# A decoder's second self-attention with four heads side by side in tiles of 32 rows, and one ring of four PSUM banks for scores and outputs in both self-attentions

## The reference

```python
# layer 0: 16 heads of 16 features, rotary positions, causal
p = softmax(where(causal, (q @ k.T) * 16 ** -0.5, -inf));  out = p @ v
# layer 1: differential attention, 16 heads, each of two half heads of 8 features
scores = einsum('bthd,bshd->bhts', qh, kh) * SCALE;  p = softmax(scores, axis=-1)
attn1, attn2 = attend(q1, k1), attend(q2, k2)          # same v for both
a = attn1 - lam * attn2;  a = a * rsqrt(mean(a * a, -1) + RMS_EPS) * rms_weight
```

## Time and profile before

| | us |
|---|---|
| runs | 3790.27, 3794.53 (median), 3812.66 |
| the profiled execution | 3793.69 |
| its span, first to last instruction | 3792.0 |
| first self-attention, from the first maximum matmul to the last reciprocal L678 | 144.1 to 629.89 |
| second self-attention, from the first reduction to the last reciprocal L678 | 1297.91 to 2641.81 |

### The profile page before, as it was taken

The page is one execution under the profiler, slowest core; times in us unless marked ns, Lnnn a source line. Parts: engine busy times, 40 slices in busy tenths (PEclk is TensorE's granted clock), DMA queues, the critical chain, the costliest instruction groups (busy, mean ns, idle before and its releaser), DMA issues. The chain is left out here.

```text
span 3792.0 us, 63919 instructions
## 1 busy us (share of the span) xinstructions
PE 3304.4 (87%) x23832; PEld 1646.7 (43%) x23832; DVE 2877.6 (76%) x4740; ACT 2100.6 (55%) x4079; POOL 912.5 (24%) x1343
## 2 busy tenths in 40 slices
PE   8499999686798799999999999999647599998748
PEld 4244444443686433333333333333424355544625
DVE  7688883467577999999999999996545377775475
ACT  3178886254232278888888888889412133333110
POOL 4233433144334300000000000000224434444000
PEclk9699998787899889999999999999778799999679
DMA  5322220000002500000100000010002311000202
GB/s 176 117 53 53 60 62 5 23 1 1 24 1 64 160 10 24 22 19 19 27 19 19 22 24 19 19 27 2 4 20 108 116 47 47 24 24 4 95 19 79
DMA packets 77548, 157.14 MB, mean 41 GB/s; under 512 B 21336, under 2 KB 38752, under 8 KB 77120
## 3 DMA queue, kind: packets, MB, share of 16 engines
q1 hardware_dynamic: 73024, 148.97, 13.1%
q10 hardware_dynamic: 4224, 4.19, 0.3%
HBM read 87.76 MB, written 54.72 MB: 38 GB/s over the span
## 5 line engine op out<-in xcount | busy, mean ns | idle before, releaser
L584 ACT ACTIVATE L_parts<-L_attn_psS 128x512 f32<-128x512 f32 (+3 forms) x2816 | 1442.6, 570 | 221.2 <-PE L_attn_psS L711 193.3
L667 DVE TENSOR_REDUCE L_attn_tops<-L_attn_psM 128x2 f32<-128x1024 f32 x1152 | 1397.8, 1222 | 95.1 <-PE L_attn_psM L761 85.1
L761 PE MATMUL L_attn_psM<-L_K,L_Q 62*128 62x512 f32 (+3 forms) x2816 | 996.4, 454 | 60.9 <-DVE L_attn_tops L667 26.8
L711 PE MATMUL L_attn_psS<-L_Q,L_K 64*128 64x512 f32 (+3 forms) x2816 | 1002.8, 439 | 1.4 <-ACT L_parts L584 1.0
L732 PE MATMUL L_attn_psO<-L_parts,L_attn_V 128*32 128x256 f32 (+1 forms) x10752 | 850.1, 388 | 20.2 <-ACT L_attn_oT L605 19.4
L711 PEld LDWEIGHTS L_attn_psS<-L_Q,L_K 64*128 64x128 f32 x2816 | 432.3, 187 | 534.7 <-ACT L_parts L584 467.5
L761 PEld LDWEIGHTS L_attn_psM<-L_K,L_Q 62*128 62x128 f32 x2816 | 415.8, 191 | 106.2 <-DVE L_attn_tops L667 58.3
L732 PEld LDWEIGHTS L_attn_psO<-L_parts,L_attn_V 128*32 128x32 f32 x10752 | 212.2, 108 | 473.7 <-issue 247.1
L661 DVE CUSTOM_DVE_ANT_0 L_attn_psM<-L_attn_psM,L_attn_wide 128x384 f32<-128x384 f32 (+3 forms) x512 | 236.6, 523 | 21.3 <-PE L_attn_psM L761 20.8
L2296 ACT ACTIVATE x_E<-x_psS 128x512 f32<-128x512 f32 x256 | 138.9, 595 | 178.4 <-PE x_psS L2419 165.7
L2342 DVE TENSOR_REDUCE x_tops<-x_psM 128x2 f32<-128x1024 f32 x128 | 153.2, 1206 | 90.0 <-PE x_psM L2448 89.9
(11 more groups left out here) (343 smaller groups left out, 4035.6 us busy)
## 6 DMA issues: line engine op xcount, KB each, us to landing
parts_q<-L_parts SPq DMA_DIRECT2D x64, 256.0 KB
parts_k<-L_parts SPq DMA_DIRECT2D x64, 256.0 KB
L_Q<-parts_q SPq DMA_DIRECT2D x192, 64.0 KB
L_K<-parts_k SPq DMA_DIRECT2D x192, 64.0 KB
L_Q<-parts_q SPq DMA_DIRECT2D x64, 128.0 KB
L_K<-parts_k SPq DMA_DIRECT2D x64, 128.0 KB
queries<-x1p_qo SPq DMA_DIRECT2D x16, 512.0 KB
keys<-x1p_ko SPq DMA_DIRECT2D x16, 512.0 KB
```

Source lines behind the costliest of these rows:

```text
L584: act.activation(E[(4 * n + s) % (4 * RING)][:, c0:], psS[bank][:, c0:], ACT.Exp, scale=scale).then_inc(e_done, 1)
L667: dve.tensor_reduce(dst, src, AX, ALU.max).then_inc(m_read, 1)
L711: pe.matmul(psS[bank][:, c0:], K[g.slot][r:r + RH, c, kt * P:(kt + 1) * P], Q[g.slot][r:r + RH, c, q * HALF + c0:(q + 1) * HALF], start=Tr ...
L761: last = pe.matmul(psM[bank][:, j * HALF:j * HALF + n], Q[t.slot][r:r + TOP, c, qt * P:(qt + 1) * P], K[t.slot][r:r + TOP, c, h * HALF:h * ...
```

## The change

Three edits, in `load_group` and `attend`.

1. In the second layer `RH` is 32: the four heads of a group lie at partitions 0, 32, 64 and 96 of chunk 0; chunk 1 is not used. `TOP` becomes 30, so a `most` contracts 30 rows instead of 62, a `score` 32 instead of 64. The DMAs are as many and as large.
2. In the second layer the list of maxima pairs alternates between heads (2, 3) and (0, 1), so that the two `most` of a half step lie on the two heads whose scores are not being made in it: scores 0, 1 go with maxima 3, 2, and scores 2, 3 with maxima 1, 0.
3. In both layers `psO` is gone and `psS` has four banks. The output sums take a bank of the ring like any other item ("O" in `taken`), hold it over a half of the queries and give it back (`left`) with the copy L605 (now L621), which counts in `e_done`. Every item takes the bank that was given back four places before it, and waits for that one count. `o_out` is gone.

```diff
@@ load_group
         for s in range(4):
-            c, r = s // 2, 64 * (s % 2)
+            rows = 64 if dh > 8 else 32
+            c, r = s * rows // P, s * rows % P
@@ attend
-    RH = 64
+    RH = 64 if causal else 32
...
-    for s in (0, 2):
-        for t, h in blocks:
-            keys = (t + 1) * P if causal else S
-            n = min(HALF, keys - h * HALF)
-            pairs.append((s, t, h, n, causal and h * HALF + n == keys))
+    order = [(s, at) for s in (0, 2) for at in blocks] if causal else [(s, at) for at in blocks for s in (2, 0)]
+    for s, (t, h) in order:
+        keys = (t + 1) * P if causal else S
+        n = min(HALF, keys - h * HALF)
+        pairs.append((s, t, h, n, causal and h * HALF + n == keys))
...
-        psS = [m.ps(f"{tag}_attn_psS{k}", HALF) for k in range(3)]
-        psO = m.ps(f"{tag}_attn_psO", HALF)
+        psS = [m.ps(f"{tag}_attn_psS{k}", HALF) for k in range(4)]
...
+                summed = (g - 1, n - LATE - BACK) if n >= LATE + BACK else (g - 2, NS + n - LATE - BACK)
+                live = 0 <= at[0] < groups
+                if live:
+                    left += [at + (s,) for s in range(4)]
+                    taken += [at + (s,) for s in range(2)]
+                if 0 <= summed[0] < groups and (summed[1] == 0 or summed[1] - 1 in ends):
+                    taken.append(("O", summed[0], steps[summed[1]][0]))
+                if live:
+                    taken += [at + (s,) for s in range(2, 4)]
...
+                if 0 <= summed[0] < groups and summed[1] in ends:
+                    left.append(("O",) + (summed[0], steps[summed[1]][0]))
...
+        bank_of = {}
+        for k, key in enumerate(taken):
+            bank_of[key] = k if k < 4 else bank_of[left[k - 4]]
+        order = {key: k for k, key in enumerate(taken)}
+        freed = {key: 4 + k + 1 for k, key in enumerate(left)}
...
-                    act.activation(oT[q][:], psO[:], ACT.Copy).then_inc(o_out, 1)
+                    act.activation(oT[q][:], psS[bank_of["O", g, q]][:], ACT.Copy).then_inc(e_done, 1)
...
-                    pe.wait_ge(e_done, i + 1)
+                    pe.wait_ge(e_done, order[g.base, n, s] + 1)
...
-                            pe.wait_ge(o_out, g.times(2, q))
+                            pe.wait_ge(e_done, order["O", at, q] + 1)
...
-                        last = pe.matmul(psO[32 * s:32 * s + 32, lo:hi], V[g.slot][:, kt, s // shared, :],
+                        last = pe.matmul(psS[bank_of["O", at, q]][32 * s:32 * s + 32, lo:hi], V[g.slot][:, kt, s // shared, :],
```

More of the change, by code:

```diff
@@ L417, in attend @@
         o_done = sems.sem(f"{tag}_attn_o_done")
-        o_out = sems.sem(f"{tag}_attn_o_out")
         o_rec = sems.sem(f"{tag}_attn_o_rec")
@@ L442, in in_turn @@
             return range(NS if new or last else LATE + BACK + 4)
-        s_at, count = {}, 0
+        taken, left, s_at = [], [], {}
         for g in range(1, groups + 2):
@@ L448, in attend @@
                 at = (g - 1, n - LATE) if n >= LATE else (g - 2, NS + n - LATE)
-                if 0 <= at[0] < groups:
-                    for s in range(4):
-                        s_at[at + (s,)] = count + s
-                    count += 4
+                summed = (g - 1, n - LATE - BACK) if n >= LATE + BACK else (g - 2, NS + n - LATE - BACK)
[7 more added lines that the diff above has]
+                    taken += [at + (s,) for s in range(2, 4)]
                 if n == 0 and last:
-                    s_at["T", g - 1] = count
-                    count += 1
+                    taken.append(("T", g - 1))
+                    left.append(("T", g - 1))
+                if 0 <= summed[0] < groups and summed[1] in ends:
+                    left.append(("O",) + (summed[0], steps[summed[1]][0]))
                 if n == BACK1 and old:
-                    s_at["B", g - 2, 1] = count
-                    count += 1
+                    taken.append(("B", g - 2, 1))
+                    left.append(("B", g - 2, 1))
                 if n == BACK0 and last:
-                    s_at["B", g - 1, 0] = count
-                    count += 1
+                    taken.append(("B", g - 1, 0))
+                    left.append(("B", g - 1, 0))
+        bank_of = {}
[3 more added lines that the diff above has]
+        freed = {key: 4 + k + 1 for k, key in enumerate(left)}
+        count = 0
+        for key in taken:
+            if key[0] != "O":
+                s_at[key] = count
+                count += 1
         def s_item(*key):
-            return s_at[key], s_at[key] % 3
+            return s_at[key], bank_of[key]
         def m_item(g, p):
@@ L535, in cut @@
                     pt = mparts[g % 3]
-                    pool.wait_ge(e_done, s_at["T", g] + 4)
+                    pool.wait_ge(e_done, freed["T", g])
                     pool.wait_ge(m_cut, 2 * g + 1)
@@ L542, in trim @@
                     for s in range(4):
-                        pool.wait_ge(e_done, s_at[g, n, s] + 4)
+                        pool.wait_ge(e_done, freed[g, n, s])
                         block = E[(4 * n + s) % (4 * RING)][:, c0:c0 + P]
@@ L567, in _ @@
             def _(act):
-                act.sem_inc(e_done, 3)
+                act.sem_inc(e_done, 4)
                 for k in range(4):
@@ L602, in evacuate @@
                 def evacuate(g, q):
-                    act.wait_ge(o_done, g.times(NS, RING + ends[q] + 1))
-                    act.activation(oT[q][:], psO[:], ACT.Copy).then_inc(o_out, 1)
+                    act.wait_ge(o_done, NS * g + RING + ends[q] + 1)
+                    act.activation(oT[q][:], psS[bank_of["O", g, q]][:], ACT.Copy).then_inc(e_done, 1)
                 def turn(t, new, last, old):
@@ L616, in turn @@
                         if old and k == BACK - 1:
-                            evacuate(t + -2, 1)
+                            evacuate(t.base - 2, 1)
                         if last and k == ends[0] + BACK:
-                            evacuate(t + -1, 0)
+                            evacuate(t.base - 1, 0)
                         if old and n == BACK1:
@@ L674, in invert @@
                 def invert(g, q):
-                    dve.wait_ge(e_done, s_at["B", g, q] + 4)
+                    dve.wait_ge(e_done, freed["B", g, q])
                     if g >= 1:
@@ L746, in turn_back @@
                     i, bank = s_item("B", g, q)
-                    pe.wait_ge(o_out, 2 * g + q + 1)
-                    pe.wait_ge(e_done, i + 1)
+                    pe.wait_ge(e_done, freed["O", g, q])
+                    pe.wait_ge(e_done, order["B", g, q] + 1)
                     for j in range(4):
@@ L768, in turn_maxima @@
                     pe.wait_ge(m_neg, g + 2)
-                    pe.wait_ge(e_done, i + 1)
+                    pe.wait_ge(e_done, order["T", g] + 1)
                     pe.transpose(psS[bank][0:4 * TB, 0:P], negm[g % 3][:], ident[:]).then_inc(s_done, 1)
```

2 lines of the change are left out of this document (1 added, 1 removed).

## The result

The changed kernel takes 3676.3 us (median of four runs, 3673.31 to 3686.62) against 3792.4 us for the kernel before beside it (four runs, 3789.46 to 3812.66): a ratio of 0.9676, 95% interval 0.9655 to 0.9697. 3675 was forecast. The profiled execution took 3676.61 us.

A forecast was written before the change was run, and what follows sets the result against it. PE, not DVE, was taken to bound the second attention's half step at 1.240 us. Savings of 107 us from four row tiles and 8 + 4 us from the shared ring, 119 in all, gave 3675 us, range 3640 to 3740.

The forecast's parts named there:

- PE binds before, by the second pair: Second attention, kernel before: PE sets the 1.240 us half step; a second score and maximum on the same rows cost 0.23.
- PE needs 1.01 us afterwards: Second attention, changed kernel: PE's need per half step, down from 1.240 us, if four row tiles run side by side.
- The tiles' term: Second attention: four row tiles save 0.109 us a half step, 3.49 us a turn, 107 us in all.
- What binds then: Second attention after the change: DVE's reductions, starting 1.131 us apart, were to bound each half step.
- loop (b): Second attention: products wait for the previous step's last exponential; 2.24 us for two half steps, just within 2.26.
- Loop (a): Second attention: a second score waits for the exponential of the previous half step's first score; 2.09 us for two half steps.
- The ring: Output sums share four score banks, so products stop waiting for the output copy: 8 us in second attention, 4 in first.
- The sum: Whole kernel: savings of 107, 8 and 4 us make 119 us, giving 3675 us.
- 1 (loop (b) binds, or a dearer set): Rival, second attention: half step 1.15 to 1.22 us instead of 1.131; 3713 us at 1.17, 3752 at 1.21; chance 0.14.
- 2 (two pairs after all): Rival, second attention: four row tiles run as two pairs, PE stays at 1.24 us; whole 3782 us; chance 0.08.
- 3 (the clock): Rival, second attention: PE's waits for DVE make its clock fall; about 3970 us if low half the time; chance 0.07.

## Why the prediction was right

The forecast came true in its main mechanism; which engine binds afterwards it named a little wrong, and some of its closeness is luck.

*PE binds before, by the second pair.* Shown: the turn doesn't move when the reduction is halved, falls to 38.09 us with the tiles alone, and to 33.70 us when the second pair goes and both other engines are shortened. *PE needs 1.01 us afterwards.* Shown, in every second half step and in the kernel with both short. The reason differs by a hair: the products start 0.43 us behind a set of four, where they start 0.33 behind the second pair; 0.43 + 0.57 = 1.00.

*The tiles' term, 3.49 us a turn, 107 in all.* The tiles alone gave 3.47. That it fits to 0.02 is partly luck. In the middle of a half a step went from 2 x 1.240 = 2.48 to 2.24 us, not to DVE's 2.26: 16 steps would give 3.84. What a turn has beyond 16 such steps grew, from 41.56 - 39.68 = 1.88 to 38.09 - 35.84 = 2.25 us, and took 0.37 back.

*What binds then* was named a little wrong. The prediction put the bound at DVE's 1.131 us and called loop (b), 2.24 against 2.26 for two, just fitting. Both sizes were met, but DVE did not bind: a short reduction gave 0.03 us a turn, a short exponential 0.90, of which loop (b) alone is 0.29. At the ends of halves ACT also has the copies, which the prediction left out of the loops; that they make up the rest is likely and not shown. DVE alone would allow 36.86 us, what goes through ACT 37.73. The time came out because DVE's pace and loop (b) are within 1% of one another in the middle of a half; a change that sped up DVE alone on the strength of the prediction would have gained 0.03 us a turn. Loop (a) was sized too small: 2.09 us with 0.33 from the pair to the products, where it is 0.43 behind a set of four and the loop 2.18. That is still under 2.26, so the sum did not suffer.

*The ring, 8 us in the second attention and 4 in the first.* In the second it is 31 x 0.33 = 10 us on top of the tiles and 31 x 0.51 = 16 alone; in the first the turn fell from 27.98 to 27.79 us and the stretch by 2.7; it is 422.3 to 423.0 us in the three profiles without the ring and 418.9 to 420.0 in ten of eleven with it. The bounds held. The middle was an arbitrary pick, and the row that it should have been weighed by is the one that grows: the wait of 0.18 us at the copy is 0.48 once PE is faster.

*The sum.* 107 + 8 + 4 = 119 forecast. The turns gave 116.5 for 107 + 8, and the 15 turns of the first attention 2.7 for 4. The rest is 2.6 less between the attentions and 4.7 more behind them. The first of these holds the last group of the first attention, 4.6 us shorter at a higher granted clock; with the ring that group takes 38.4 to 45.1 us from profile to profile and without it 41.7 to 43.1, so the gain is not the change's by any evidence here. What lies behind the last reciprocal is not touched by the change and grew by 5.3 us, with 11 us more at the lower clock. That these parts nearly cancel is luck.

*Rivals.* 1 (loop (b) binds, or a dearer set): loop (b) does come ahead of DVE in the middle of a half, but at 2.24 / 2 = 1.12 us a half step, under the 1.15 at which this rival began; the set of four lasts 0.50 us, as one. The Trainium skill's "TensorE: Matmul & The Clock Gate", section "Measured speedup vs the span model", has 3.07 times for four row tiles, by which the prediction estimated a half step of PE at 1.16 us; the trace has 1.01, so that estimate does not hold for this stream. 2 (two pairs after all): refuted by the starts within 0.01 us. 3 (the clock): did not come in nine executions of the changed kernel, which came to 1.00 in the first turn with scores in both traces. But its price was right (1.74 for 1.73), and it is no fancy: with the pair order as it was, it came in three of five executions (a fourth, 3723.73 us at a mean clock of 0.898, lies between), and with it reversed in all four. The prediction looked for it in the waits for DVE. That was the wrong place: in the two traces that stayed low PE read busy for 593 of 595 us and for 2235 of 2235. The same page's section "A second HAM failure mode: psum-queue depth-cycling" blames short idle times between groups for a clock that swings; in the kernel with later turns the clock fell twice, each time right behind a wait of PE of 1.40 or 1.44 us for a DMA, which agrees, but that the wait was the cause was not tested. The long stretches at the lower clock are not of that kind, for they have no such waits.

So of the pair order the prediction said the lesser half. At full clock it is worth 0.4 us a turn against the old order. Its larger worth is that in every execution seen the clock comes up.

## What to carry to other kernels

Take an engine's need from the starts of its instructions, not from its busy share, and shorten one engine's work at a time to see which binds: DVE read 95% busy, and halving it moved nothing. Where matmuls use only part of the rows, order them so that the ones that can run together lie on as many different row tiles as there are. With the order reversed, neighbours in the stream still lay on different tiles, but on two instead of four. Here this paid twice, in time and in the clock. And try the order both ways and several times: a schedule that looks equal in work can be 29% slower, or slow in some executions only.

## What was not expected of the hardware

- PE can read busy almost throughout and stay at 1.2 GHz: for 2235 of 2235 us with two matmuls of 32 rows at a time, and for 593 of 595 us of one execution with two and four in turn (in the second case the gaps all lie before 1353 us, where maxima are still made alone). With 64 + 64 rows, or with four tiles in every half step, every profiled execution came to 2.4 GHz within 51 us of the end of turn 0. Why is left open.
- Four matmuls on four row tiles last as long as one, 0.50 us at 2.4 GHz and 0.79 at 1.2. The products start 0.43 us behind a set of four and 0.33 us behind a set of two. A second set on the same rows adds 0.23 us to a half step at 2.4 GHz and 0.42 at 1.2.
- A reduction of 1024 elements lasts 1.22 us, but the next can start 1.13 us after its start. So DVE reads as busy throughout at any half step up to 1.22 us, though it could follow one of 1.13.
